# Self attention whose tiles run on across turns, with the output product in the value projection's bank

## What is computed

```
q = (h @ wq), k = (h @ wk), v = (h @ wv)          # h: the modulated layer norm of x, 128 -> 16 x 64
scores = einsum('bhqd,bhkd->bhqk', q, k) / sqrt(64)
attn   = softmax(scores, axis=-1)
x = x + einsum('bhqk,bhkd->bhqd', attn, v) @ wo + bo
```

## Time and profile before

| what | value |
|---|---|
| runs | 2917.85, 2904.52, 2907.86 us, median 2907.86 |
| span of the profiled execution | 2915.3 us; the longest of the three runs is 2.55 us above it |
| the self attention stage, with its barriers | 50.0 to 594.6 us of the span |
| busy in the span | PE 2481.6 us (85%), DVE 1903.1, ACT 1576.6, POOL 991.5 |
| one turn of the stage | 16.66 us, 32 of them |

### The profile page before, as it was taken

One profiled execution on the slowest core, in us unless ns is written; L12 is line 12 of the kernel. 1 busy time (PEld: TensorE's weight loads), 2 busy tenths in 40 slices (PEclk: granted clock), 3 DMA queues, 4 the chain that ended last, 5 costly groups with the idle time before them and its releaser, 6 DMA issues. The chain is left out here.

```text
span 2915.3 us, 137471 instructions
## 1 busy us (share of the span) xinstructions
PE 2481.6 (85%) x57411; PEld 1686.9 (58%) x57412; DVE 1903.1 (65%) x7219; ACT 1576.6 (54%) x5266; POOL 991.5 (34%) x1992
## 2 busy tenths in 40 slices
PE   7999999987897799889899898898879877666669
PEld 4666666666455455556565565666656545444448
DVE  4666666775442477767777677777767766776553
ACT  4666666633353366666666576666657543333322
POOL 2000000043010167645677465566636411001125
PEclk9999999999898899999999999999999999999989
DMA  4000000000001200001100011000001000000013
GB/s 150 5 5 5 5 5 8 2 12 1 9 19 46 60 17 18 14 21 42 28 18 17 11 36 35 26 13 14 7 7 35 13 20 7 6 7 7 6 48 85
DMA packets 51896, 64.76 MB, mean 22 GB/s; under 512 B 7432, under 2 KB 36560, under 8 KB 51152
## 3 DMA queue, kind: packets, MB, share of 16 engines
q1 hardware_dynamic: 47184, 50.32, 5.8%
q0 software_dynamic: 4096, 5.67, 1.0%
HBM read 46.38 MB, written 9.60 MB: 19 GB/s over the span
## 5 line engine op out<-in xcount | busy, mean ns | idle before, releaser
L2267 POOL TENSOR_TENSOR gru_terms<-gru_states,gru_signs 128x8 f32<-128x8 f32 x512 | 103.3, 202 | 796.5 <-DVE gru_states L2552 690.2
L2008 PE MATMUL gru_ps_sr<-score_w,gru_states 128*32 128x78 f32 x4096 | 175.4, 243 | 184.0 <-DVE gru_states L2552 174.1
L2187 ACT ACTIVATE gru_p_t<-gru_ps_tc,gru_negmax 128x12 f32<-128x12 f32 x512 | 138.4, 270 | 338.4 <-DVE gru_negmax L2521 319.5
L2190 ACT ACTIVATE gru_th_r<-gru_pre_r 128x32 f32<-128x32 f32 x512 | 119.2, 233 | 303.8 <-DVE gru_pre_r L2534 303.6
L2243 POOL TENSOR_SCALAR bg_probs<-bg_probs,bg_arsum 128x256 f32<-128x256 f32 (+2 forms) x192 | 240.5, 1253 | 84.8 <-DVE gru_c_in L2541 78.7
L1758 PE MATMUL gru_ps_tc<-ctx_gate_w,gru_p_t 128*4 128x64 f32 x12288 | 267.6, 219 | 1.2 <-issue 1.2
L371 ACT ACTIVATE self_probs<-self_sc,self_negmax 128x512 f32<-128x512 f32 x256 | 174.2, 684 | 166.2 <-DVE self_negmax L428 166.2
L1758 PE MATMUL gru_ps_sr<-ctx_gate_w,gru_p_t 128*4 128x34 f32 x12288 | 189.5, 194 | 76.9 <-ACT gru_p_t L2187 74.2
L2008 PEld LDWEIGHTS gru_ps_sr<-score_w,gru_states 128*32 128x32 f32 x4096 | 81.1, 107 | 293.5 <-DVE gru_states L2552 275.6
L1758 PEld LDWEIGHTS gru_ps_sr<-ctx_gate_w,gru_p_t 128*4 128x4 f32 x12288 | 120.2, 86 | 195.4 <-ACT gru_p_t L2187 179.4
L2020 PE MATMUL gru_ps_ox<-late,gru_states 128*4 128x128 f32 x4096 | 225.5, 272 | 0.0
(11 more groups left out here) (417 smaller groups left out, 6599.9 us busy)
## 6 DMA issues: line engine op xcount, KB each, us to landing
bg_w<-in_moe_w SPq DMA_DIRECT2D x48, 256.0 KB, 3.1
bg_wa<-in_wqkv SPq DMA_DIRECT2D x24, 192.0 KB, 2.4
moe_w<-in_moe_w SPq DMA_DIRECT2D x16, 256.0 KB, 3.7
best_w_sb<-in_ec_w SPq DMA_DIRECT2D x16, 256.0 KB
x_products<-late SPq DMA_DIRECT2D x16, 240.0 KB, 2.4
late<-x_products SPq DMA_DIRECT2D x240, 16.0 KB
cross_scratch<-ctab_raw SPq DMA_DIRECT2D x16, 154.0 KB
cross_outs<-cross_scratch POOLq DMA_DIRECT2D x4, 576.0 KB, 5.9
```

The costliest lines, as they stand in the source:

```text
L2008: last = pe.matmul(ps_s[32 * b:32 * b + 32, :], state(t)[:, b:b + 1].broadcast_to([P, 32]), score_w[:, b, 0:CTX + 1], start=True, stop=Tru ...
L2187: act.activation(p_t[:], ps_t, ACT.Exp, bias=negmax[:, 0:1]).then_inc(s_exp, 1)
L2190: act.activation(th_r[:, 1:64:2], pre_r[:], ACT.Tanh, scale=0.5).then_inc(s_thr, 1)
```

## The change

A function `self_attention` takes the place of `attention` (whose branches for masks and norms, used by nobody, go), with the same work in another order:

- On all three engines a turn no longer ends with its last tiles. Transposes of tile 3 and value products of tiles 2 and 3 of turn it - 1 now stand between the scores of turn it. ScalarE's copies and VectorE's copy of ot move with them.
- Scores are issued one tile at a time, four times a turn, where tiles 0 and 1 stood together.
- The output product goes into the bank of the value projection, now called vw, and no longer into ot. So `values` waits for the copy of ot to o_sb (s_oe) and not for the addition to y; `project_v` waits for the addition to y of the turn before the last; `project_out` waits also until v was copied out.
- v is projected at the end of the turn before, and v_sb has two places, by turn.
- Each wait is written at each call. Of the rows in TensorE's list that carry more than one wait there are 12 in a turn before (8 transposes, 1 scores, 1 values, q/k, output product) and 19 now (8 transposes, 4 scores, 4 values, q/k, v, output product). All but one wait of such a row is an instruction of its own.
- VectorE handles one tile at a time: two maxima, two scalings. In the last pair the statistics of finished rows stand before the maxima of tile 3, where they stood behind them.

```diff
--- before
+++ after
-        q_sb, k_sb, v_sb = sb("q_sb", [P, S]), sb("k_sb", [P, S]), sb("v_sb", [P, NT, P])
+        q_sb, k_sb, v_sb = sb("q_sb", [P, S]), sb("k_sb", [P, S]), sb("v_sb", [P, 2, NT, P])
...
-        ot, vb = pb("ot"), pb("vb")
+        ot, vw = pb("ot"), pb("vw")
...
                 sp.wait_ge(s_pv, pair * B)
+                sp.wait_ge(s_pk, pair * B)
...
+            def project_qk(it):
+                pe.wait_ge(s_w, pair_of(it) * 16 + 16)
                 wait_positive(pe, s_exp, it * U - 2)
-                pe.matmul(sc[0][:], w_sb[:, 0, :], tokens(b), start=True, stop=True).then_inc(s_pq, 1)
-                pe.matmul(sc[1][:], w_sb[:, 1, :], tokens(b), start=True, stop=True).then_inc(s_pk, 1)
-
-            def project_v(it, b):
-                wait_positive(pe, s_ve, it)
+                pe.matmul(sc[0][:], w_sb[:, 0, :], tokens(it), start=True, stop=True).then_inc(s_pq, 1)
+                pe.matmul(sc[1][:], w_sb[:, 1, :], tokens(it), start=True, stop=True).then_inc(s_pk, 1)
+
+            def project_v(it):
+                pe.wait_ge(s_w, pair_of(it) * 16 + 16)
+                wait_positive(pe, s_y, it - 1)
                 for kt in range(NT):
-                    last = pe.matmul(vb[:, kt * P:(kt + 1) * P], tokens(b)[:, kt * P:(kt + 1) * P], w_sb[:, 2, :],
-                                     start=True, stop=True)
+                    last = pe.matmul(vw[:, kt * P:(kt + 1) * P], tokens(it)[:, kt * P:(kt + 1) * P], w_sb[:, 2, :], start=True, stop=True)
                 last.then_inc(s_pv, 1)
 
-            def square_sums(it):
-                wait_positive(pe, s_exp, it * U)
-                for i in range(2):
-                    wait_positive(pe, s_sq, it * 2 + i + 1)
+            def project_out(it):
+                pe.wait_ge(s_oe, it + 1)
+                pe.wait_ge(s_ve, min(it + 2, N))
+                pe.wait_ge(s_wo, pair_of(it) * 16 + 16)
+                for j in range(NT):
+                    last = pe.matmul(vw[:, j * P:(j + 1) * P], o_sb[:, j * P:(j + 1) * P], wo_sb[:], start=True, stop=True)
+                last.then_inc(s_wd, 1)
...
+            def values(it, n):
+                pe.wait_ge(s_pte, it * U + 2 * n + 2)
+                pe.wait_ge(s_ve, it + 1)
+                wait_positive(pe, s_oe, it)
...
-            turns(pe, turn)
+            project_qk(0)
+            project_v(0)
+            for it in range(N):
+                scores(it, 0)
+                if it:
+                    turn_probs(it - 1, 3)
+                    values(it - 1, 2)
+                scores(it, 1)
+                turn_probs(it, 0)
+                if it:
+                    values(it - 1, 3)
+                scores(it, 2)
+                turn_probs(it, 1)
+                if it:
+                    project_out(it - 1)
+                values(it, 0)
+                scores(it, 3)
+                turn_probs(it, 2)
+                if it + 1 < N:
+                    project_qk(it + 1)
+                values(it, 1)
+                if it + 1 < N:
+                    project_v(it + 1)
+            turn_probs(N - 1, 3)
+            values(N - 1, 2)
+            values(N - 1, 3)
             turn_rows(0)
-            project_out(NP * B - 1, NP - 1)
+            project_out(N - 1)
...
-                act.activation(v_sb[:], vb[:].rearrange("p (t d) -> p t d", d=P), ACT.Copy).then_inc(s_ve, 1)
+                act.activation(v_sb[:, it % 2, :, :], vw[:].rearrange("p (t d) -> p t d", d=P), ACT.Copy).then_inc(s_ve, 1)
...
-            turns(act, turn)
+            take_v(0)
+            for it in range(N):
+                exponentials(it, 0)
+                if it:
+                    take_turned(it - 1, 3)
+                exponentials(it, 1)
+                take_turned(it, 0)
+                exponentials(it, 2)
+                take_turned(it, 1)
+                exponentials(it, 3)
+                take_turned(it, 2)
+                if it + 1 < N:
+                    take_qk(it + 1)
+                    take_v(it + 1)
+            take_turned(N - 1, 3)
...
+            def take_out(it):
+                dve.wait_ge(s_ot, it + 1)
+                wait_positive(dve, s_wd, it)
+                dve.tensor_copy(o_sb[:], ot[:]).then_inc(s_oe, 1)
...
+            for it in range(N):
+                known = it > (NP - 1) * B
+                maxima(it, 0)
+                normalise(it, 0)
+                maxima(it, 1)
+                normalise(it, 1)
+                if it:
+                    take_out(it - 1)
+                maxima(it, 2)
+                normalise(it, 2)
+                if it:
+                    add_out(it - 1)
+                if known:
+                    moments(it - 1 - (NP - 1) * B)
+                maxima(it, 3)
+                normalise(it, 3)
+                if known:
+                    scale_rows(it - 1 - (NP - 1) * B)
+            take_out(N - 1)
+            add_out(N - 1)
```

More of the change, by code:

```diff
@@ L136, in wait_positive, with self_attention, pair_of, tokens @@
         eng.wait_ge(sem, n)
[L139 to L167, removed]
+def self_attention(nc, spent, name, h_cols, y, wqkv, wo, weights, ident, out_bias, q_scale, on_pool, then):
+    N, U = NP * B, 2 * NT
+    def pair_of(it):
+        return it // B
+    def tokens(it):
+        return h_cols[:, it % B * S:(it % B + 1) * S]
     with ExitStack() as ctx:
@@ L191, in attention @@
         s_y0 = sem("y0")
[L192 to L195, removed]
         eps, cols_out, scale, shift = then
@@ L264, in scores @@
-                    last = pe.matmul(sc[u % 4][:, 0:keys(n)], q_sb[HD * j:HD * j + HD, tile(n) * P:(tile(n) + 1) * P],
-                                     k_sb[HD * j:HD * j + HD, 0:keys(n)], start=True, stop=not causal)
-                    if not causal:
-                        last.then_inc(s_sc, 1)
-                if causal:
-                    for j in range(2):
-                        pe.matmul(sc[(2 * n + j) % 4][:, keys(n) - P:keys(n)], masks[0], masks[1], start=False, stop=True)\
-                          .then_inc(s_sc, 1)
+                    half = slice(HD * j, HD * j + HD)
@@ L279, in turn_probs @@
+                    wait_positive(pe, s_pte, u - 1)
+                    for kt in range(NT):
                         last = pe.transpose(pt[j][:, kt * P:(kt + 1) * P], probs[:, u % 4, kt * P:(kt + 1) * P], ident)
@@ new lines, in normalise @@
+            def normalise(it, n):
+                for u in (2 * n, 2 * n + 1):
+                    dve.wait_ge(s_exp, it * U + u + 1)
+                    dve.reciprocal(rtotal[:, u:u + 1], total[:, u:u + 1]).then_inc(s_rt, 1)
+                    dve.wait_ge(s_rt, it * U + u + 1)
+                    row = probs[:, u % 4, :]
+                    dve.tensor_scalar(row, row, rtotal[:, u:u + 1], None, ALU.mult).then_inc(s_pn, 1)
+            def take_out(it):
+                dve.wait_ge(s_ot, it + 1)
+                wait_positive(dve, s_wd, it)
+                dve.tensor_copy(o_sb[:], ot[:]).then_inc(s_oe, 1)
@@ L499, in _ @@
-            if out_bias is None:
-                dve.memset(y[:], 0.0).then_inc(s_y0, 1)
-                dve.wait_ge(s_y0, 1)
-            else:
-                dve.tensor_tensor(y[:], y[:], out_bias.rearrange("p (a d) -> p a d", a=1).broadcast_to([P, B * NT, P]),
-                                  ALU.add).then_inc(s_y0, 1)
-                dve.wait_ge(s_y0, 1)
-            if norm is not None:
-                scale_qk(0, 0)
-            dve.memset(n_power[:], -0.5).then_inc(s_npower, 1)
-            turns(dve, turn)
```

220 lines of the change are left out of this document (39 added, 181 removed).

## The result

The changed kernel takes 2897.64 us (median of 20 runs, 2890.48 to 2905.21). The kernel before, run 20 times in the same way, takes 2914.49. The ratio is 0.9945, 95% interval 0.9936 to 0.9954: 16.9 us or 0.55% faster. The forecast was a gain of 15.8 us and 2892.1 us; the gain is met within what these runs can tell (the interval is 13.4 to 18.7 us), and the absolute time lies 5.5 us above the forecast because the median of the kernel before moved from 2907.86 with 3 runs to 2914.49 with 20.

The account below looks back on a forecast made before the run. TensorE, with small holes, bounds the stage. A turn goes from 16.66 to 16.14 us; 32 x 0.52 = 16.6, less 0.8, is 15.8 us, taking the median 2907.86 to 2892.1 us, range 2882 to 2903.

Parts of the forecast that it names:

- TensorE's pure work: TensorE's work in one turn without holes or changes of kind: 13.90 us, with visits priced on top.
- The holes go: TensorE's waits at tile 0's second-head transposes and value product vanish, -1.18 us a turn; added visits cost +0.66.
- The margins of the walk: New order timed from profiled durations; margins 0.3 us at transposes of tile 0, 0.4 at output product, 0.6 at next scores.
- Output product's bank: The output product's move to v's bank lets old values 3 stand behind scores 1; no time of its own.
- Second place of v: Two places in v_sb: claimed the same as the output product's bank, no time of its own.
- SyncE's loads: Pair weights asked for at the end of the turn before, due some 12 us later; free.
- Added wait instructions: In TensorE's list, 19 wait instructions a turn for 12, each 51 ns long; taken to cost zero.
- Statistics in the last pair: VectorE's statistics delay maxima of tile 3 by about 1.0 us, 0.4 beyond margin in two turns: +0.8 us.
- The ends: First turn lacks three groups of a turn before, which follow the last turn instead; even, within 1 us.
- Against the median: The 15.8 us gain was subtracted from the three-run median, 2907.86, giving 2892.1 us.
- Rival 1: The gain comes, but the rest of the program hides part: 2 to 6 us, 2894 to 2898; chance 0.20.
- Rivals 2, 3 and 4: 2: one close wait late, 2903, chance 0.15; 3: kind changes free, 2870, 0.03; 4: added waits cost, 2911 to 2923, 0.06.

Follow-up runs that it names:

- run 20: Not a label of a run: the words say the kernel before was run 20 times, like the changed kernel; its median is 2914.49 us.
- old_bank: The changed kernel with the output product back in ot's bank, VectorE adding to y behind the scaling of tile 2; 2991.19 us.
- late_copy: The changed kernel with ScalarE's copies of old tile 3 moved behind the exponentials of tile 1; 3026.18 us, one run.
- old_bank_early_add: The changed kernel with the output product in ot's bank and the addition to y ahead of the scaling of tile 2; 2925.03 us.
- one_v_place: The changed kernel with one place for v, copied by ScalarE in its own turn behind the copies of tile 0; 2895.09 us.

## Why the prediction was right, point by point

- *TensorE's pure work, 13.90 us, and 0.15 to 0.2 a visit.* Right. It predicted the turn of the changed kernel as 16.14 (measured 16.13) and, in the experiments, 16.32 (16.33), 15.92 (15.93) and 15.32 (15.33), all turns in which TensorE never waits.
- *The holes go, -1.18, and four visits come, +0.66.* Right. old_bank, late_copy and old_bank_early_add bring a hole back by the wait that the walk names, and its length follows: 2.05 expected and 2.04 to 2.09 measured, 2.8 and 2.84, 0.85 and 0.87.
- *The margins of the walk.* Right, and to 0.1 us. The ends of three copies in the turn from 407.04:

```profile
410.27 1.08 ACT L320 ACTIVATE self_probs_t<-self_pt 128x512 f32<-128x512 f32 x2
...
414.11 0.68 DVE L360 COPY self_o_sb<-self_ot 128x512 f32<-128x512 f32 x1
...
421.91 0.62 ACT L305 ACTIVATE self_k_sb<-self_sc 128x512 f32<-128x512 f32 x1
```

The first copy of old tile 3 is over after some 0.60 us, at 410.87, and the transposes begin at 411.21: 0.34, where the walk had 0.3. ot is copied at 414.79, the output product begins at 415.24: 0.45 for 0.4. k is copied at 422.53, the next scores begin at 423.17: 0.64 for 0.6. The walk therefore holds event by event, and the turn is not right by errors that cancel. late_copy shows what stands behind the first margin; the one at the output product was not tried.
- *Output product's bank: needed, no gain of its own.* Right on both, in the two forms tried.
- *Second place of v "the same", needed by the order.* Wrong in that word: the order runs as fast with one place.
- *SyncE's loads, free.* Right: the turns in which a pair of heads ends are 16.12 or 16.13 us like the others.
- *Added wait instructions, zero.* Right.
- *Statistics in the last pair, +0.8.* Measured 0.91. In the timeline of the changed kernel the first scores of the last two turns, and the last transposes:

```profile
536.50 1.13 PE L236 MATMUL self_sc<-self_k_sb,self_q_sb 64*128 64x512 f32 x4 [0.37 <-issue]
...
553.10 1.13 PE L236 MATMUL self_sc<-self_k_sb,self_q_sb 64*128 64x512 f32 x4 [0.40 <-issue]
...
568.25 1.12 PE L244 MATMUL self_pt<-early,self_probs 128*128 128x128 f32 x8 [1.76 <-ACT self_probs_t L320]
```

The two rows with "issue" are the late copies of k: the waits were met only then, though the trace names no engine. The turns that end there are 16.57 and 16.60 us.

- *The ends, even within 1 us.* Mis-sized in this execution. Two things stand behind it. First, the third turn with statistics has no next turn, and the prediction put its delay at nothing. It shows in the last transposes, which wait 1.76 us for ScalarE's copies [the last row above]. ScalarE makes these copies behind the exponentials of tile 3, and those start late; the rows are of the turn from 407.04 and of the last one, from 553.10:

```profile
419.14 0.69 ACT L314 ACTIVATE self_probs<-self_sc,self_negmax 128x512 f32<-128x512 f32 x1 [1.30 <-DVE self_negmax L347]
...
566.17 0.69 ACT L314 ACTIVATE self_probs<-self_sc,self_negmax 128x512 f32<-128x512 f32 x1 [2.27 <-DVE self_negmax L347]
...
567.51 1.08 ACT L320 ACTIVATE self_probs_t<-self_pt 128x512 f32<-128x512 f32 x2
```

They begin 12.10 us after the first scores in the one and 13.07 in the other, so 0.97 of the 1.76 us is the delay of the statistics. From its first scores to the end of the stage the last turn takes 1.7 us more than before.

Second, the first turn, which lacks the four groups that belong to a turn before it, is only 0.33 us shorter than the others; in one_v_place it is 14.96 us, 1.17 shorter. In the changed kernel's trace a stretch there runs at the lower clock. One row of the timeline, one window, and a window of one_v_place:

```profile
59.56 1.94 PE L244 MATMUL self_pt<-early,self_probs 128*128 128x128 f32 x8 [0.51 <-ACT self_probs_t L320]
```
```profile
59.20:62.60 3.40, 3.04 (x26) 2.56 (x28) 2.93 (x7) 3.02 (x8) 0.00 (x0) 0.66 1.04 286
```
```profile
59.00:63.00 4.00, 3.56 (x32) 2.42 (x33) 3.31 (x9) 3.59 (x9) 0.00 (x0) 1.00 1.02 287
```

The granted clock is 0.66 in the first window and 1.00 in the second. TensorE's idle times ahead of it are the same in both traces (1.45 us, then 0.25 and 0.23), so they do not decide it alone; what does was not tried. The ends cost 1.7 - 0.33 = 1.4 us here, and 1.7 - 1.17 = 0.5 us where the first turn keeps the upper clock, within the 1 us that was forecast.
- *Against the median.* The sum was subtracted from a median of three runs, which lay 6.6 us below that of twenty. That the profiled execution was above the median by 7.4 us set its span against a median of three times. A time is some 1.8 to 2.5 us above its span, so a span of 2915.3 is a time near 2917.5, which is 3 us above the median of twenty. Part of the agreement is luck: the stage from its first scores on gives 14.1 us, the sum had 15.8, and the medians of the whole program say 16.9. All three lie inside the interval of 13.4 to 18.7 us, so these runs do not tell them apart. In the text on the range 0.2 x 32 is 6.4; the 7 us follow from a third of 0.66.
- *Rival 1* (the rest of the program hides part) can't be seen: the rest was 1.5 us shorter in the profiled execution, and its length in the other profiles lies between 2309 and 2319 us, a spread that would cover a loss of 2 to 6 us. *Rivals 2, 3 and 4* fell: no wait is late, changes of kind are not free, wait instructions are.

## What to carry to other kernels

Where one engine bounds a stage that is repeated, list its groups with their distances from start to start, in every neighbourhood that the trace has: the difference between a group alone and two in a row is the price of changing the kind of matmul. Then write the new order down as a walk with margins; it gave every turn here without a hole to 0.02 us, and the turn with a hole of 0.87 us to 0.11. Filling holes by finer interleaving buys changes of kind, 0.66 of 1.18 us here; work that fills a hole should be of the kind of its neighbour, and the order with the fewest visits of those tried, which still covers the waits, brought more than twice the gain.

## What was not expected of the hardware

A hole on TensorE can be paid twice. In kernels with idle time of 2.04 to 2.09 us or 2.84 us each turn the granted clock fell again and again to the lower level, 1.2 GHz, for some 3.5 us while the following groups ran (0.55 from 390.40 to 393.90; means of 0.94 and 0.92 over 200 and 400 us), and these turns were 1.5 to 1.6 us longer than the hole alone explains. It fell in 20 of 30 turns with the hole of 2.04 to 2.09 us, and in every turn from the third on with the one of 2.84. With 0.87 us each turn, or the 0.22 and 0.67 us of the kernel before, it stayed at 1.00 in the middle of the stage. Old_bank lost some 32 us to this (20 turns, 1.6 us each) beside some 65 us of holes (31 turns, 18.24 - 16.13 each), so a walk that gives a long hole gives only a lower bound of its cost.
